# Multi-head attentions of a four-layer stack: the four groups of weighted values of a sequence move into one run behind the next sequence's scores

## The reference

```
x = x + tanh(g_xattn[i]) * attention_i(layernorm(x), ctx_1024, ...)
x = x + tanh(g_ffn[i])   * ffn_i(layernorm(x), ...)
```

```
q, k, v = heads(Query @ Wq + bq), heads(Key @ Wk + bk), heads(Values @ Wv + bv)
scores  = einsum('bhqd,bhkd->bhqk', q, k) / sqrt(16)      # layer 0: masked
attn    = softmax(scores)
out     = einsum('bhqk,bhkd->bhqd', attn, v) @ Wo + bo
```

## Time and profile before

| what | value |
|---|---|
| time, median of 3 runs | 1744.72 us (1743.67 to 1747.17) |
| profiled execution: its span, first to last instruction | 1741.7 us |
| PE busy / PEld / DVE / ACT / POOL over the span | 95% / 74% / 64% / 57% / 55% |
| granted TensorE clock, mean over the span | 0.996 |
| L0x, PE from the first scores (25.31) to the last (182.22) | 16 rounds, from the fifth on 10.60 and 10.76 us by turns |
| L2x, the same from 1154.78 to 1298.60 | from the fifth on 9.73 and 9.90 us by turns |
| L3x, the same from 1569.68 to 1716.71 | from the fifth on 10.05 us |

### The profile page before, as it was taken

The page is one execution under the profiler, slowest core; times in us unless marked ns, Lnnn a source line. Parts: engine busy times, 40 slices in busy tenths (PEclk is TensorE's granted clock), DMA queues, the critical chain, the costliest instruction groups (busy, mean ns, idle before and its releaser), DMA issues. The chain is left out here.

```text
span 1741.7 us, 38448 instructions
## 1 busy us (share of the span) xinstructions
PE 1660.0 (95%) x11910; PEld 1293.1 (74%) x11910; DVE 1117.6 (64%) x3319; ACT 1000.9 (57%) x2824; POOL 955.9 (55%) x1182
## 2 busy tenths in 40 slices
PE   7999799989889999999999999999998999999998
PEld 4778488858547777777777777768876888867886
DVE  4787776637556666666667666547885353337875
ACT  4677455547436665666665666448782355537775
POOL 2356676558455566555555555333777244457762
PEclk9999999999999999999999999999999999999999
DMA  4333286565200000000000000013435345432200
GB/s 157 97 101 121 85 253 202 160 233 176 109 7 4 4 4 6 4 4 4 4 4 6 4 4 4 5 50 107 137 141 187 89 126 145 139 134 74 77 26 25
DMA packets 79668, 140.27 MB, mean 81 GB/s; under 512 B 11728, under 2 KB 61104, under 8 KB 77296
## 3 DMA queue, kind: packets, MB, share of 16 engines
q1 hardware_dynamic: 65744, 98.22, 18.1%
q0 software_dynamic: 13728, 39.60, 6.4%
HBM read 84.88 MB, written 50.82 MB: 78 GB/s over the span
## 5 line engine op out<-in xcount | busy, mean ns | idle before, releaser
L1596 POOL TENSOR_TENSOR L1f_rn<-L1f_ss,L1f_root_c 128x8 f32<-128x8 f32 x64 | 105.5, 1648 | 184.3 <-DVE L1f_ss L1899 181.8
L1732 PE MATMUL L1f_psQ<-L1f_xT,arena 128*128 128x128 f32 x1408 | 172.4, 275 | 0.9 <-ACT L1f_xT L1807 0.9
L1732 PEld LDWEIGHTS L1f_psQ<-L1f_xT,arena 128*128 128x128 f32 x1408 | 169.5, 192 | 4.4 <-ACT L1f_xT L1807 1.1
L1825 ACT ACTIVATE L1f_sg<-L1f_psQ,vec1f 128x128 f32<-128x128 f32 x192 | 63.4, 364 | 138.0 <-PE L1f_psQ L1732 136.8
L2125 POOL DMA_INDIRECT outs_L2f<-L2f_tiles_ys,L2f_tiles_spot x79 | 75.8, 960 | 119.5 <-ACT L2f_tiles_ys L2273 104.3
L1611 POOL TENSOR_TENSOR L1f_rot<-L1f_qn,L1f_sinT 128x512 f32<-128x512 f32 x64 | 113.0, 1786 | 29.0 <-DVE L1f_qn L1915 29.0
L1945 DVE SCALAR_TENSOR_TENSOR L1f_hid<-L1f_psQ,vec1f,L1f_sg 128x128 f32<-128x128 f32 x192 | 61.2, 346 | 90.1 <-ACT L1f_sg L1825 89.6
L1656 PE MATMUL L1f_psQ<-arena,L1f_hT 128*128 128x512 f32 x256 | 118.4, 605 | 0.6 <-ACT L1f_hT L1814 0.6
L1744 PE MATMUL L1f_psB<-arena,L1f_hid 128*128 128x256 f32 (+1 forms) x384 | 99.7, 388 | 0.0
L2125 POOL DMA_INDIRECT outs_L0f<-L0f_tiles_ys,L0f_tiles_spot x79 | 75.9, 961 | 43.0 <-ACT L0f_tiles_ys L2273 34.8
L1601 POOL TENSOR_TENSOR L1f_pr<-L1f_pr,L1f_rs 128x512 f32<-128x512 f32 x64 | 95.6, 1514 | 6.2 <-DVE L1f_rs L1909 6.2
(11 more groups left out here) (535 smaller groups left out, 4705.6 us busy)
## 6 DMA issues: line engine op xcount, KB each, us to landing
L0f_tiles_xs<-rows_L0f SPq DMA_DIRECT2D x79, 144.0 KB
L2f_tiles_xs<-rows_L2f SPq DMA_DIRECT2D x79, 144.0 KB, 2.2
arena<-in_w_L2f SPq DMA_DIRECT2D x8, 1120.0 KB, 5.8
arena<-in_w_L1f SPq DMA_DIRECT2D x8, 1088.0 KB, 7.3
L1x_got<-outs_L0f SPq DMA_DIRECT2D x16, 512.0 KB, 3.9
L3x_got<-outs_L2f SPq DMA_DIRECT2D x16, 512.0 KB, 3.3
arena<-in_w_L0f SPq DMA_DIRECT2D x8, 768.0 KB, 4.7
rows_L0f<-zero SPq DMA_DIRECT2D x31, 144.0 KB
```

Of the source, the lines that this page charges most:

```text
L1596: nc.gpsimd.tensor_tensor(rn[:, s.p, h], ss[:, s.p, h], root_c[:, 0:LH], ALU.pow).then_inc(s_rn, 1)
L1732: mm = nc.tensor.matmul(out, w, xT[:, k], start=(k == 0), stop=(k == KC - 1), skip_group_check=True)
L1825: nc.scalar.activation(sg[to, u], unit_out(u, 0, of), ACT.Gelu, bias=column(s, 2 * KC + u)[of]).then_inc(s_sg, 1)
```

## The change

In PE's list of a round, and nowhere else, `weigh(0)` and `weigh(1)` leave their place between `keys` and `turn(2)`, and stand one round later directly behind `scores` together with `weigh(2)` and `weigh(3)`. All four groups then precede `logits`, which stood between `scores` and `weigh(2)` before. No instruction is added or removed; each wait travels with its piece. ACT, DVE, POOL and SP keep their lists.

```diff
-            each_round([(ready_table, -7)] * ready + [(scores, 0)] + [(logits, -4)] * (route is not None)
-                       + [(at(weigh, 2), -1), (at(weigh, 3), -1), (values_in, 1)] + [(soon(rank), -5)] * (route is not None)
+            each_round([(ready_table, -7)] * ready + [(scores, 0)] + [(at(weigh, g), -1) for g in range(4)]
+                       + [(logits, -4)] * (route is not None) + [(values_in, 1)] + [(soon(rank), -5)] * (route is not None)
                        + [(filtered, -4)] * (store is not None)
                        + [(output, -2), (turn_back, -1)] + [(route_turn, -3), (late(rank), -4)] * (route is not None)
                        + [(filter_turn, -3)] * (store is not None)
-                       + [(turn_in, 2), (at(turn, 1), 0), (at(turn, 0), 0), (turn_out, -1), (keys, 2), (at(weigh, 0), 0),
-                          (at(weigh, 1), 0), (at(turn, 2), 0), (at(turn, 3), 0), (queries, 2)], low_t, high_t)
+                       + [(turn_in, 2), (at(turn, 1), 0), (at(turn, 0), 0), (turn_out, -1), (keys, 2), (at(turn, 2), 0), (at(turn, 3), 0), (queries, 2)], low_t, high_t)
```

## The result

The changed kernel takes 1759.58 us (median of four runs, 1757.42 to 1761.1), the kernel before, beside it, 1744.26: ratio 1.0076, 95% interval 1.0057 to 1.0096. The forecast was 1754 with a range of 1746.5 to 1760. A ratio in this text is the recorded estimate, which leaves out one run of 3916 us of the kernel before, and not the quotient of two medians, which here would be 1.0088. Direction and rounds came as forecast.

What follows compares the result with a forecast made beforehand. PE sets the pace with ACT's chain 0.42 us behind; the late logits' copy makes ACT bind. 4.2 + 4.2 + 1.4 - 1.4 + 0.75 = 9.2 us on the 1741.7 span, plus 3.0 to the median: 1754, range 1746.5 to 1760.

Steps and rivals of the forecast that it cites:

- PE's own work gets shorter by 0.4 to 0.6: PE's round: 0.84 leaves behind the keys, 0.45 returns in the longer run; 0.4 saved, 0.6 in rounds with logits.
- The further 0.2 for rounds with logits: PE, rounds with logits: one more going in and out of a run saved, since values follow logits without one; 0.2 us.
- The logits' copy comes 1.0 later, ACT swallows its idle 0.19, keys' copy ends at 106.81, next scores 0.50 later: ACT's chain in L0x and L2x rounds from the fifth on: 0.50 us later a round, 0.34 in rounds with rank.
- both waits arrive together: L0x round on PE: turn(3), ready to end at 106.85, and the keys' copy, ending at 106.81, hold the queries alike.
- The first place to wait is the queries, with 0.42 of slack: PE's queries wait for ACT's keys' copy; that chain is 0.42 us shorter than PE's own work, 0.61 with idle place.
- Rounds 4 to 13: 4.2, 4.2 and 1.4: Ten rounds each with logits or filter: us lost in L0x, L2x and L3x; in L3x +0.14 a round through filter_turn.
- First rounds -1.4: Rounds 0 to 3, without logits: round 0 nothing, rounds 1 to 3 about 0.15 gained each, -0.45 per attention.
- Last rounds +0.75: Round 14 and the last round: late exponentials and logits' copy cost +0.45 in L0x, +0.4 in L2x, -0.1 in L3x.
- The rival of the falling clock: PE idles some 0.7 us in each of 20 rounds, so half-clock stretches add 10 us: 1764; 4 in 100.
- Cancelling: Slacks each 0.3 longer than read: L0x and L2x gain 2 us, L3x and first rounds give back: 1742 to 1748; 13 in 100.
- PE's order decides: PE's saving of 0.4 or 0.6 comes out in every round, 21 us faster: 1724; 8 in 100.

Runs made afterwards that it cites:

- the copy behind the exponentials: Changed kernel with ACT's copy of the logits moved behind the exponentials of group 1, PE's order untouched; 1754.69 us, ratio 1.0049 against the kernel before.
- logits alone: Kernel before with only the logits moved, behind weigh(2) and weigh(3); weigh(0) and weigh(1) stay behind the keys; 1750.44 us, ratio 1.0029.
- the first series: First timing of the changed kernel beside the kernel before: 1759.58 against 1744.26 us, ratio 1.0076.
- the filled kernels: Changed kernel and kernel before, each with spare matmuls behind the last scores of L0x and L2x: 1753.54 us (1.0039) and 1744.56 us (0.9993).
- the second series: Changed kernel timed again beside the kernel before, together with the moved logits and the spare matmuls: 1757.15 against 1745.38 us, ratio 1.0059.
- the one with the moves: Changed kernel with logits ahead of the run of four and transposes of routed and filtered rows earlier: 1745.52 us (0.9993); with spare matmuls 1739.66 (0.9961).

## Why the prediction was right, and where it was not

- *PE's own work gets shorter by 0.4 to 0.6.* Right in L0x with 0.48: the run of four is 1.01 long where 1.02 was reckoned, and the place behind the keys gave back 0.84. The further 0.2 for rounds with logits was too much; from logits to values it is 0.46 where logits to `weigh(2)` took 0.55, so 0.09.
- *The logits' copy comes 1.0 later, ACT swallows its idle 0.19, keys' copy ends at 106.81, next scores 0.50 later.* Right, to 0.03. Counted from the start of the scores the keys' copy was to end after 9.14 and ends after 9.11; the round was to be 11.10 and is 11.11. Shown by the copy behind the exponentials, which takes 0.36 of the 0.43 away. That both waits arrive together, `turn(3)` and the queries, was right too: with the copy moved, `turn(3)` alone keeps PE's saving from coming out. In L2x 10.24 came for 10.24 (9.90 + 0.34).
- *The first place to wait is the queries, with 0.42 of slack.* Wrong, without harm to the sum. The smallest slack is that of `turn(0)`, which waits for `route_in`: 0.12. Half the delay already costs 0.24 a round (logits alone). Both waits end in the same chain on ACT, so its length set the round either way. Taken as a free delay of 0.42 it gives 20 x (0.58 - 0.42) = 3 us for the logits alone, where 5.1 came.
- *Rounds 4 to 13: 4.2, 4.2 and 1.4.* The sums of the ten distances grew by 4.3, 4.4 and 1.8. In L3x 0.18 a round came for 0.14; ACT's idle time ahead of the filter's copy grew from 0.33 to 0.77, the 0.44 of the longer run.
- *First rounds -1.4.* -2.2 came (0.20, 0.22, 0.25 in rounds 1 to 3 of L0x, where 0.15 each were taken): the wait that I feared there cost less than that.
- *Last rounds +0.75.* This is the term that failed: the whole sum was short by 6.1 us in the first series and by 2.6 in the second, and the distances, with 8.9 us, were not what it lacked. The last distances (+0.22 in L0x and L2x each, +0.06 in L3x) and the wait for the logits' copy (0.36 in place of 0.2) were about right, and between the filled kernels the stretches behind the last scores differ by 0.70 and 0.82 only. Missing was the granted clock in those stretches: the changed kernel's trace has 4.5 us more there, an estimated 5.1 of it work at half clock, and 3.6 us come back with nothing but spare matmuls. That the change lowers the clock there is not shown beyond the traces: over all runs of the second series the two kernels have the same mean clock and still lie 11.8 us apart, of which 2.9 are outside the distances and unexplained. That 1759.58 still lay in the range, 0.4 from its end, owes something to luck.
- *The rival of the falling clock* had the right mechanism in the wrong place. It was put into the 20 steady rounds, where PE idles for 0.3 to 0.5 us a round, and there, in the steady rounds of L0x and L2x, the clock stayed 1.00. The earlier trace rows held the clue: the stretch at 0.55 lies behind the last scores. Its price of up to 1.5 us each was fair (four such stretches more, an estimated 5.1 us); it belonged into the term of the last rounds, not into a rival at 4%.
- *Cancelling, and PE's order decides.* Both fell. The second would have been the rule of the Trainium skill ("Perfetto Trace Analysis", Identifying the Most-Contended Engine), which calls the engine with the highest occupancy the most contended and says to optimize it first. PE is at 95%, and its work was shortened. The trace disagrees: 0.48 less work a round of L0x gave 0.35 to 0.51 more time.

What stays open is the share of the clock in the 2.9 to 6.8 us outside the distances, and whether the change is what lowers it. The filling takes 3.6 us away in the changed kernel and 5.9 in the one with the moves, costs PE some work itself, and leaves some half-clock stretches.

## What to carry to other kernels

A step's slack is that of the first wait behind it in each queue it passes through, a bank that must be free as much as a value that must be there; walk every release down the queue before taking the longest chain as the only one. When an edit touches a pipeline, reckon the stretch behind its last round by itself, with the granted clock that it has now, and over several executions: it has no work left that hides a wait, and one trace does not tell its clock. And an edit that shortens the busiest engine pays only with the steps around it moved: here the run of four cost 0.6 to 0.8% alone. It gave nothing that can be measured with the logits ahead of it and the two transposes earlier, and 0.4% with the last stretch filled as well (1739.66 against 1745.67 us).

## What the runs showed of the chip

- A run of float32 matmuls of 32 output rows each (128 columns, each recorded twice) costs 1.01 us for 16 of them and 0.57 for 8 at full clock, so about 0.44 for each further 8 and 0.13 for the run itself.
- Spare matmuls of 256 columns, 52 at the end of L0x and 40 at the end of L2x, made the changed kernel 3.6 us and the re-ordered one 5.9 us faster; in the kernel before they changed nothing that can be measured. The mean granted clock rose in all three.
- The same program took 1744 to 1746 us in four series of runs and 1794 in one, with the same undisturbed rounds to 0.02 us. What differed in that series is not known. The profiles show its extra time above all in the stretch of layer 0's experts and layer 1 (953 to 956 us, where others have 935 to 939.5) and in that from L2x's experts to L3x (252 to 255 against 245 to 246). More of it lies behind the last scores of L0x and L2x, with waits of 4 to 7 us and a lower clock, and in late rounds of L2x.
